# A decoder layer with sixteen experts: the expert stage reads its tiles' experts and names sixteen to a register load in place of four

## The chip, the cores and the metric

The kernel runs on one core of a Trainium2 chip. The metric is the device time of one execution in microseconds (us), the median of several runs, lower is better. Five engines work beside each other and meet at semaphores: TensorE (PE: matrix products; the profile lists its weight loads apart as PEld), VectorE (DVE), ScalarE (ACT), GpSimd (POOL) and SyncE (SP, which here only issues transfers). Each has a sequencer that takes its instructions in order. Instructions that work on registers are carried out by the sequencer itself and are not counted as busy time; the profile lists them for a line of the kernel under PEldq and SPq.

## The reference

One decoder layer over 2048 rows of width 256, in float32, with a layer norm after each of three parts:

```python
x = _layernorm(x + attention(x))                 # linear attention, 8 heads
x = _layernorm(x + cross_attention(x, ctx))      # 16 heads, 1601 keys
x = _layernorm(x + ffn(x))                       # mixture of experts
# ffn:
probs = softmax(xf @ gate_w.T)                   # 16 experts
top_w, top_idx = top_k(probs, 4);  top_w /= sum(top_w)
h1 = einsum('td,ehd->teh', xf, w1);  h3 = einsum('td,ehd->teh', xf, w3)
eout = einsum('teh,edh->ted', silu(h1) * h3, w2)
moe_out = einsum('ted,te->td', eout, combine)    # combine: the four weights of a row
shared = silu(xf @ sw1.T) * (xf @ sw3.T) @ sw2.T
out = moe_out + shared
```

## The kernel before

Attention and cross attention take the first 750 us of the trace. The change is in what comes after, the expert stage.

**Tiles.** The 2048 x 4 choices are sorted by expert into tiles of 128 rows, `SLOT_TILES` = 79 of them, which a row of DRAM (`sorted_d`) holds. Which expert a tile belongs to is known only on the chip. VectorE works out an order of the tiles and writes for each place in it two integers, the place of the expert's weights in `w_all` and the name (number) of the tile. They go through DRAM into `order_row`, on one partition of on-chip memory, in two versions: version 0 is complete for the first 48 places (`KNOWN_OWNERS`), version 1 for all.

**Work.** `WORK` is a fixed list of 95 items: 16 tiles of the shared expert ("s") and the 79 expert tiles ("e", place v): `"s"*4 + "e"*8 + "se"*6 + "e"*65 + "s"*6`. Every engine walks through it by the same index i, with a software pipeline. TensorE does at step i, in this order: a job of the last rows' attention and gate, if `LAST` has one for this i; `turn_rows(i+3)` (two transposes of the tile's rows, line 1601); `inner(i+1)` (products with w1 and w3, line 1639); `turn_act(i-1)` (one transpose, line 1647); `outer(i-3)` (product with w2, line 1657). For a place v that is a multiple of `EXPERT_LOAD`, `inner` first calls `load_owners(v)`, which reads `EXPERT_LOAD` integers of `order_row` into registers of TensorE with the instruction TENSOR_LOAD (line 1611). With four to a load that is at 20 places: v = 0, 4, ... 76, the last with three integers. The products then address the weights by register (`bass.ds(owners[v] + n, 1)`), for which the sequencer runs a FUSED_REGOPS for each. `inner(i)` waits for two things ahead of that: the tile's transposed rows (`xT_copied`, from ScalarE) and the activations of item i-2 (`act_ready`, from VectorE, line 2180).

**ScalarE, VectorE, GpSimd.** ScalarE copies the transposes out (1141, 1155), takes silu of the first product (1145) and scales the result (1163); VectorE multiplies (2180); GpSimd scatters a tile's 128 result rows to `given_d` in DRAM (874). Later VectorE adds four given rows for each row, normalises, and the result is stored.

**SyncE.** It issues the loads of the expert tiles' rows, `load_tile(i+8)` at step i (`X_AHEAD`), 14 of them ahead of the loop, each addressed by a register (line 695). At places that are a multiple of `EXPERT_LOAD` it first reads as many tile names (`name_tiles`, line 671). The very first read, for v = 0, is at the last step of cross attention, ahead of the wait for the sorted rows (line 679). Into its 18 buffers (`X_SLOTS`) a tile may go only when the tile 18 places before it has been given out. From step 63 on SyncE issues the loads of the given rows too, and the stores.

Places and steps: v = 0 is item 4, v = 16 item 26, v = 32 item 42, v = 48 item 58, v = 64 item 74.

Of the kernel before, what the change touches and what calls it, by code (L numbers as in the profile page):

```python
# [112 lines left out]
ACT_SLOTS = 3  # L113
WHOLE_SILU = 10
X_AHEAD = 8
EXPERT_LOAD = 4
IDLE_PRODUCTS = 3
EK_RING = 4
XQ_RING = 2
# [17 lines left out]
assert SLOT_TILES <= LISTED <= P and X_SLOTS % Y_SIGNALS == 0 and Y_SLOTS % Y_SIGNALS == 0  # L137
assert len(WORK) == TILES + SLOT_TILES and KNOWN_OWNERS % EXPERT_LOAD == 0
assert LASTK > 0 and REST * TPC <= CHUNK and UNITS == PER_STEP * KT


def decoder_layer(nc, a, out):
    with ExitStack() as ctx:
# [369 lines left out]
        def _(sp):  # L513
# [152 lines left out]
            def name_tiles(v):  # L666


                n = min(EXPERT_LOAD, SLOT_TILES - v)
                sp.wait_ge(order_in, 16)  # L670
                _, got = nc.values_load_multi_w_load_instructions(
                    order_row[0:1, 0, v:v + n, 1], engines=[mybir.EngineType.SP], min_val=0, max_val=SLOT_TILES - 1,
                    skip_runtime_bounds_check_because="the order is a permutation of the tiles")
                for k in range(n):
                    tile_at[v + k] = got[k]
# [5 lines left out]
            def load_tile(i):  # L681
                kind, v = WORK[i]
                if kind == "expert":
                    if v % EXPERT_LOAD == 0 and v:
                        name_tiles(v)
# [548 lines left out]
        def _(pe):  # L1234
# [371 lines left out]
            def load_owners(v):  # L1606


                n, known = min(EXPERT_LOAD, SLOT_TILES - v), int(v >= KNOWN_OWNERS)
                pe.wait_ge(order_in, 16 * (known + 1))  # L1610
                _, got = nc.values_load_multi_w_load_instructions(
                    order_row[0:1, known, v:v + n, 0], engines=[mybir.EngineType.PE], min_val=0,
                    max_val=W_PARTS * (EXPERTS + W_GAP - 1),
                    skip_runtime_bounds_check_because="a count of experts, cut off at the last one")
                for k in range(n):
                    owners[v + k] = got[k]
# [6 lines left out]
            def inner(i):  # L1623
# [5 lines left out]
                else:  # L1629
                    if v % EXPERT_LOAD == 0:  # L1630
                        load_owners(v)
# [750 lines left out]
```

## Time and profile before

| | |
|---|---|
| median of 3 runs | 959.58 us (958.43 to 962.15) |
| span of the profiled execution | 955.3 us |
| TensorE busy in it | 896.6 us (94%) |
| expert stage | about 750 to 955 us |
| register loads | 20 on TensorE, 20 on SyncE |

The span runs from the first to the last instruction of the profiled execution and is the only time of it that is listed; 4.3 us of the median of the runs lie outside it. Times within the trace count from the start of the span. In the table of waits and in the timeline "idle before <- releaser" is the time an engine stood still and the instruction of another engine whose end let it go on.

### The profile page before, as it was taken

How to read it: one execution, taken by the hardware profiler on the slowest of the kernel's cores; microseconds unless marked ns; L12 is line 12 of the kernel's file. 1: busy time of each engine (PE TensorE's matmuls, PEld its weight loads, DVE VectorE, ACT ScalarE, POOL GpSimd, SP SyncE). 2: the span in 40 equal slices, each digit the busy share in tenths (PEclk: the TensorE clock that was granted, in tenths of full speed). 3: DMA queues.
4: the chain of work that ended last, by engine and by line, in shares of the span. 5: the costliest groups of instructions: out<-in, count | busy, mean ns of one | idle time of the engine just before them, and what ended most of it. 6: DMA issues, size and time to landing. Idle time of an engine off the chain costs nothing.

```text
span 955.3 us, 18981 instructions
## 1 busy us (share of the span) xinstructions
PE 896.6 (94%) x6843; PEld 514.1 (54%) x6843; DVE 710.7 (74%) x1138; ACT 660.4 (69%) x1491; POOL 303.4 (32%) x355
## 2 busy tenths in 40 slices
PE   9998999799999999999999999999989997889995
PEld 5776876344444444444444444444433475677874
DVE  5324879899999998989998989988897271311477
ACT  4434574268888888878888878876779763556654
POOL 1608886600000000210000200023444446555574
PEclk9999999979999999999999999999999999999997
DMA  9207847502343400100100100102335433344795
GB/s 323 80 1 143 128 129 130 126 25 89 94 136 116 129 15 23 30 9 25 31 9 23 31 8 25 30 25 79 102 120 164 127 116 127 109 136 155 240 305 184
DMA packets 69839, 93.07 MB, mean 97 GB/s; under 512 B 15254, under 2 KB 52632, under 8 KB 69686
## 3 DMA queue, kind: packets, MB, share of 16 engines
q1 hardware_dynamic: 62068, 70.06, 26.7%
q0 software_dynamic: 6928, 18.82, 5.2%
q10 hardware_dynamic: 752, 2.98, 1.9%
q8 instruction: 56, 0.92, 0.4%
q14 instruction: 35, 0.29, 0.1%
HBM read 50.34 MB, written 39.40 MB: 94 GB/s over the span
## 4 chain that ended last, share of the span: by engine, by line
PE 75%; DVE 13%; ACT 4%; issue 3%; another core or an unknown queue 2%; POOL 2%; DMA 1%; POOLq 0%; DVEq 0%; SPq 0%; ACTq 0%
PE psum L1456 20%; PE psum L1364 16%; PE psum L1442 9%; PE psum L1639 8%; DVE mpart L1813 8%; PE psum L1657 3%; PE psum L1288 2%; PE psum L1383 2%; PE psum L1253 2%; ACT region L1191 2%; PE psum L1601 2%; PE psum L1314 2%; PE psum L1416 2%; PE psum L1478 1%
## 5 line engine op out<-in xcount | busy, mean ns | idle before, releaser
L1191 ACT ACTIVATE region<-psum 128x512 f32<-128x512 f32 (+1 forms) x832 | 448.4, 610 | 99.4 <-PE psum L1442 83.0
L1813 DVE TENSOR_REDUCE mpart<-psum 128x2 f32<-128x1024 f32 x384 | 461.8, 1222 | 33.5 <-PE psum L1364 25.8
L1456 PE MATMUL psum<-region 128*32 128x256 f32 (+1 forms) x3120 | 249.2, 391 | 2.3 <-ACT numT L1087 0.7
L1364 PE MATMUL psum<-kstack,qstack 63*128 63x512 f32 (+1 forms) x1024 | 213.9, 445 | 14.7 <-DVE mpart L1813 12.5
L1364 PEld LDWEIGHTS psum<-kstack,qstack 63*128 63x128 f32 x1024 | 88.9, 185 | 184.0 <-issue 130.8
L1442 PE MATMUL psum<-qstack,kstack 64*128 64x512 f32 (+1 forms) x832 | 176.0, 409 | 0.8 <-DMA qstack<-max_d 0.4
L1456 PEld LDWEIGHTS psum<-region 128*32 128x32 f32 (+1 forms) x3120 | 62.0, 108 | 110.8 <-issue 81.6
L1442 PEld LDWEIGHTS psum<-qstack,kstack 64*128 64x128 f32 (+1 forms) x832 | 111.8, 182 | 17.1 <-ACT region L1191 11.8
L939 POOL TENSOR_TENSOR attnT<-num_c,den_c 128x512 f32<-128x512 f32 x7 | 9.0, 1280 | 324.5 <-DMA den_c<-den_d 324.5
L1639 PE MATMUL psum<-w_all,xT_in 128*128 x316 | 84.5, 390 | 16.2 <-DVE act_h L2180 15.7
L874 POOL DMA_INDIRECT given_d<-y_out,x_in x79 | 78.3, 991 | 63.6 <-ACT y_out L1163 45.2
L2180 DVE SCALAR_TENSOR_TENSOR act_h<-silu_h,psum 128x128 f32<-128x128 f32 x95 | 27.1, 286 | 92.5 <-ACT silu_h L1145 50.9
L1639 PEld LDWEIGHTS psum<-w_all,xT_in 128*128 128x128 f32 x316 | 54.4, 192 | 24.9 <-issue 20.5
L837 POOL DMA_INDIRECT sorted_d<-x_rows,slots x48 | 47.5, 990 | 36.8 <-PE psum L1442 27.0
L1145 ACT ACTIVATE silu_h<-psum 128x128 f32<-128x128 f32 x85 | 24.6, 289 | 46.5 <-PE psum L1639 32.5
L1141 ACT ACTIVATE xT_in<-psum 128x256 f32<-128x256 f32 x95 | 37.2, 393 | 16.7 <-PE psum L1601 13.4
L1657 PE MATMUL psum<-w_all,actT 128*128 x158 | 47.7, 384 | 0.0
L1163 ACT ACTIVATE y_out<-psum,x_in 128x256 f32<-128x256 f32 x79 | 38.3, 484 | 6.9 <-PE psum L1657 3.6
L1060 ACT ACTIVATE region<-psum,small 128x64 f32<-128x64 f32 x128 | 27.9, 331 | 15.2 <-DVE small L1824 15.0
L1809 DVE TENSOR_REDUCE mpart<-psum 128x8 f32<-128x528 f32 x32 | 22.6, 708 | 12.0 <-PE psum L1364 10.6
L1155 ACT ACTIVATE actT<-psum 128x128 f32<-128x128 f32 x95 | 27.4, 288 | 5.0 <-remote 2.7
L1601 PE MATMUL psum<-ident,x_in 128*128 128x128 f32 x158 | 30.6, 275 | 0.3 <-ACT x2T L1126 0.3
(291 smaller groups left out, 1010.9 us busy)
## 6 DMA issues: line engine op xcount, KB each, us to landing
x_in<-sorted_d SPq DMA_DIRECT2D x79, 129.0 KB
sorted_d<-x_in SPq DMA_DIRECT2D x6, 1548.0 KB, 8.0
given<-given_d SPq DMA_DIRECT2D x16, 512.0 KB
qstack<-qparts_d SPq DMA_DIRECT2D x96, 64.0 KB, 2.3
qparts_d<-region SPq DMA_DIRECT2D x8, 512.0 KB, 3.3
kparts_d<-region SPq DMA_DIRECT2D x4, 800.5 KB, 12.1
kstack<-kparts_d SPq DMA_DIRECT2D x6, 400.2 KB, 10.1
kstack<-kparts_d ACTq DMA_DIRECT2D x6, 400.2 KB, 14.3
```

The lines of the kernel that those rows point to most:

```text
L837: pool.indirect_dma_start(out=sorted_d[:, :], out_offset=bass.IndirectOffsetOnAxis(ap=slots[:, t, j:j + 1], axis=0), in_=row, in_offset=No ...
L874: pool.indirect_dma_start(out=given_d[:, :], out_offset=bass.IndirectOffsetOnAxis(ap=x_in[:, v % X_SLOTS, DIM:DIM + 1].bitcast(I32), axis= ...
L1141: act.activation(xT_in[:, i % 3, :], turn_bank("tile", i)[:, 0:DIM], ACT.Copy).then_inc(xT_copied, 1)
L1163: act.activation(y_out[:, v % Y_SLOTS, :], bank(2 + i % 2)[:, 0:DIM], ACT.Copy, scale=x_in[:, v % X_SLOTS, DIM + 1:DIM + 2]).then_inc(y_co ...
L1191: act.activation(prob[0:rows_of, s % 3, j, :], ring(n)[0:rows_of], ACT.Exp).then_inc(ring_read, 1)
L1364: mm = pe.matmul(bank(unit_bank(u) + side)[:, at * w:(at + 1) * w], qstack[rows_of, buffer(G), p, t * P:(t + 1) * P], kstack[rows_of, g * ...
L1442: pe.matmul(ring(n)[0:r], kstack[rows, g * PAIRS + p, kt * P:kt * P + r], qstack[rows, buffer(G), p, :], start=True, stop=True).then_inc(r ...
L1456: mm = pe.matmul(bank(NUM_BANK)[VW * j:VW * (j + 1), q], vals[0:r, g, kt, j, :], prob[0:r, s % 3, j, q], start=(kt == 0 and half == 0), st ...
L1601: mm = pe.transpose(turn_bank("tile", i)[:, k * P:(k + 1) * P], rows[:, k * P:(k + 1) * P], ident[:, :])
L1639: mm = pe.matmul(bank(6 + i % 2)[:, 0:2 * HID], xT_in[:, i % 3, k * P:(k + 1) * P], part_of(kind, v, k), start=(k == 0), stop=(k == DK - 1))
L1657: pe.matmul(bank(2 + i % 2)[:, 0:DIM], actT[:, i % ACT_SLOTS, :], part_of(kind, v, DK), start=True, stop=True).then_inc(y_done, 1)
L1813: dve.tensor_reduce(mpart[:, G % 2, qt, :, p, n], both, X, ALU.max).then_inc(max_read, 1)
```

## The change

One constant. `load_owners` and `name_tiles` take `n = min(EXPERT_LOAD, SLOT_TILES - v)` integers wherever v is a multiple of it, so TensorE and SyncE read at v = 0, 16, 32, 48 and 64, with 16, 16, 16, 16 and 15 integers. 48 is a multiple of 16 as of 4, so version 1 of the order is used from the same place on. Nothing else is moved.

```diff
@@ -113,7 +113,7 @@
 ACT_SLOTS = 3
 WHOLE_SILU = 10
 X_AHEAD = 8
-EXPERT_LOAD = 4
+EXPERT_LOAD = 16
 IDLE_PRODUCTS = 3
 EK_RING = 4
 XQ_RING = 2
```

## Rows read from the trace of the kernel before

**Rows 1.** The page: busy time of the engines
```profile
PE 896.6 (94%) x6843; PEld 514.1 (54%) x6843; DVE 710.7 (74%) x1138; ACT 660.4 (69%) x1491; POOL 303.4 (32%) x355
```

**Rows 2.** The page: shares of the chain that ended last, by engine
```profile
PE 75%; DVE 13%; ACT 4%; issue 3%; another core or an unknown queue 2%; POOL 2%; DMA 1%; POOLq 0%; DVEq 0%; SPq 0%; ACTq 0%
```

**Rows 3.** Waits of TensorE, 755 to 940 us (total, times, longest)
```profile
PE psum L1639 <- DVE act_h L2180: 15.7, 14, 4.1
```

**Rows 4.** Lines 1611 and 671 over the whole span (min/median/max ns)
```profile
L1611 PEldq TENSOR_LOAD <-order_row x20: 757/1147/1345, 762.6 to 925.6; - x20
...
L671 SPq TENSOR_LOAD <-order_row x20: 861/868/1216, 750.3 to 913.7; - x20
```

**Rows 5.** Line 1611, single loads, each in a window around it
```profile
L1611 PEldq TENSOR_LOAD <-order_row x1: 1188/1188/1188, 762.6 to 762.6; - x1
...
L1611 PEldq TENSOR_LOAD <-order_row x1: 1227/1227/1227, 813.9 to 813.9; - x1
...
L1611 PEldq TENSOR_LOAD <-order_row x1: 1219/1219/1219, 846.6 to 846.6; - x1
...
L1611 PEldq TENSOR_LOAD <-order_row x1: 1160/1160/1160, 875.2 to 875.2; - x1
...
L1611 PEldq TENSOR_LOAD <-order_row x1: 1345/1345/1345, 903.6 to 903.6; - x1
...
L1611 PEldq TENSOR_LOAD <-order_row x1: 988/988/988, 918.4 to 918.4; - x1
...
L1611 PEldq TENSOR_LOAD <-order_row x1: 757/757/757, 925.6 to 925.6; - x1
```

**Rows 6.** Line 1639 on the sequencer of TensorE, either side of a load
```profile
L1639 PEldq FUSED_REGOPS  x2: 51/53/55, 874.5 to 874.6; - x2
...
L1639 PEldq FUSED_REGOPS  x2: 51/53/55, 876.6 to 876.8; - x2
```

**Rows 7.** Timeline of TensorE: first products of the tile after a load
```profile
764.54 1.13 PE L1639 MATMUL psum<-w_all,xT_in 128*128 x4 [0.35 <-DVE act_h L2180]
...
815.43 0.82 PE L1639 MATMUL psum<-w_all,xT_in 128*128 x2
...
848.45 1.13 PE L1639 MATMUL psum<-w_all,xT_in 128*128 x4 [0.36 <-DVE act_h L2180]
...
875.99 1.03 PE L1639 MATMUL psum<-w_all,xT_in 128*128 x4
...
877.61 1.03 PE L1639 MATMUL psum<-w_all,xT_in 128*128 x4
...
879.75 1.13 PE L1639 MATMUL psum<-w_all,xT_in 128*128 x4 [0.35 <-DVE act_h L2180]
...
905.45 1.03 PE L1639 MATMUL psum<-w_all,xT_in 128*128 x4
```

**Rows 8.** Timeline of TensorE: its four longest idle times here
```profile
798.03 1.33 PE L1639 MATMUL psum<-w_all,xT_in 128*128 x4 [2.51 <-DVE act_h L2180]
...
812.25 1.89 PE L1639 MATMUL psum<-w_all,xT_in 128*128 x4 [4.15 <-DVE act_h L2180]
...
825.78 1.12 PE L1639 MATMUL psum<-w_all,xT_in 128*128 x4 [1.82 <-DVE act_h L2180]
...
856.98 0.48 PE L1639 MATMUL psum<-w_all,xT_in 128*128 x1 [1.76 <-DVE act_h L2180]
```

**Rows 9.** Windows after two of these: busy times by engine, PEclk, DMA share
```profile
798.80:802.20 3.40, 3.40 (x11) 2.62 (x10) 0.72 (x3) 1.52 (x5) 2.72 (x3) 0.50 0.23 79
...
812.50:815.90 3.40, 3.40 (x11) 2.56 (x11) 0.94 (x3) 1.42 (x6) 2.08 (x3) 0.50 0.12 46
```

**Rows 10.** Line 671 on SyncE, its first and its seventeenth load
```profile
L671 SPq TENSOR_LOAD <-order_row x1: 1062/1062/1062, 750.3 to 750.3; - x1
...
L671 SPq TENSOR_LOAD <-order_row x1: 865/865/865, 893.8 to 893.8; - x1
```

**Rows 11.** Line 679 on SyncE, the wait for sorted rows
```profile
L679 SPq EVENT_SEMAPHORE  x2: 17/22/28, 755.5 to 758.5; - x2
```

## The prediction

> **What bounds the kernel now.** I read the page first. TensorE is busy 896.6 of 955.3 us [rows 1], and three quarters of the chain that ended last are its own [rows 2]. The expert stage is no exception: a tile there takes 1.62 us, from 875.99 to 877.61 [rows 7], and between 755 and 940 us TensorE waits 15.7 us in all, each time ahead of the first product of a tile and each time by the profile for VectorE's activation [rows 3]. So whatever holds TensorE up in this stage lengthens the kernel one for one, and nothing that only relieves another engine can shorten it by more than those 15.7 us.
>
> The register loads are not in this busy time. They are found by their lines: 20 on TensorE, 0.757 to 1.345 us each, median 1.147, and 20 on SyncE, median 0.868 [rows 4]. The question is what a load of sixteen integers takes, and how much of one is hidden.
>
> **The price of a load.** The trace before has one load that isn't of four integers, the last one on TensorE, of three. It took 0.757 us, the load of four before it 0.988, and no load of four in the trace was shorter than that [rows 4, 5]. The difference is 0.231 us for one integer, and 0.757 / 3 is 0.252: the time is nearly proportional to the integers, with next to nothing left for the instruction (0.757 - 3 x 0.231 = 0.064). SyncE's median of 0.868 is 0.217 for each. From this, sixteen integers cost on TensorE at least 0.064 + 16 x 0.231 = 3.8 us, and at most four times what the loads of four took at these places, 4.6 to 4.9 us (4 x 1.160 to 4 x 1.227) [rows 5]. I take 4.3, and 4.0 for the fifteen at v = 64; on SyncE 4 x 0.868 = 3.5. So the change takes away no load time worth the name: 79 integers are read either way. It gathers them in five blocks. The other end of what one short sample allows is a price for the instruction alone, 1.15 us whatever it reads; that is a rival below.
>
> The Trainium skill bears on this twice and says two things. "Runtime: NRT & Kernel Launch" (Instruction fetch mechanics) puts such a load at about 200 ns for each register, in bulk too; an estimate from it is 16 x 0.2 = 3.2 us a load, and the slope above and SyncE's 0.217 agree with it. "DMA: Bandwidth & Descriptors" (Latency and other measured facts) gives it a floor of about 600 ns and says that the compiler reads four at once to amortize that; by that rule sixteen at once would be better still, and the 0.064 us left over above speaks against it.
>
> **How much of a load is hidden.** TensorE's sequencer runs ahead of its array by the instructions that are queued. For v = 48: the load starts at 875.2 [rows 5], while the array is about to start the products of the tile before (875.99), and the next tile's products start at 877.61 without idle time [rows 7]. The sequencer's FUSED_REGOPS for those products come at 876.6 [rows 6], 0.26 us behind the load's end (875.23 + 1.16 = 876.39), and the one for the tile before came at 874.5, so the array could have waited until about 0.1 us before 877.61. The load could thus have lasted 2.0 us (877.61 - 875.23 - 0.26 - 0.1) before the array went idle: the 1.16 us are hidden, the 4.3 us are not. What hides a load is the sequencer's lead of about a tile and a half, and this can't grow, as the next tile but one has to wait for the activation of the one just computed.
>
> For each of the five loads, the start of the next products becomes load start + load time + 0.36, and the delay is what this lies behind its start now [rows 5, 7]:
> - v = 0: the four weight waits behind the load make it about 0.5 in place of 0.36: 762.6 + 4.3 + 0.5 = 767.4 against 764.54: 2.9
> - v = 16: 813.9 + 4.66 = 818.5 against 815.43: 3.1
> - v = 32: 846.6 + 4.66 = 851.3 against 848.45: 2.9 (0.36 of idle time stands there already)
> - v = 48: 875.23 + 4.66 = 879.9 against 877.61: 2.3, of which some 0.5 is taken back, since the next tile now waits at 879.75 [rows 7] and then no longer would: 1.8
> - v = 64: 903.6 + 4.0 + 0.36 = 908.0 against 905.45: 2.6
>
> The sum is 13.3 us. With 3.8 and 3.6 us a load it is 10.9, with 4.9 and 4.6 it is 16.3. Queued behind a load on TensorE is everything of the stage, from the last rows' attention on (the load at v = 0 comes ahead of their gate), and ScalarE, VectorE and GpSimd wait for it tile by tile; nothing catches up later, because the tiles that follow run at TensorE's own rate.
>
> **What the fifteen loads that go give back.** Hidden loads are worth nothing. Exposed, they can only be in the 15.7 us. Of these, 2.51 and 4.15 us end at 798.03 and 812.25 [rows 8], ahead of the loads at 799 and 813.9, and no load stands in them. The rest is 9.0 us, and that is the upper bound. 1.82 and 1.76 of it [rows 8] and ten waits that together make 5.5 us follow a load by some microseconds, with VectorE named as the releaser and not the sequencer. Whether the load has a part in them the trace doesn't settle. I take back half of the 5.5, 2.5 us (bounds 0 and 9.0).
>
> **The clock.** After the waits of 2.51 and 4.15 us the array ran at half its clock (granted 0.50, the 1.2 GHz level) for 3.4 us each time [rows 8, 9], which costs about 1.7 us; no fall follows the wait of 1.82 us. The new idle times, 2.3 to 3.3 us, lie just where it begins to happen. I put in one fall out of five, 1.7 us (bounds 0 and 5 x 1.7 = 8.5).
>
> **SyncE.** Its first load (v = 0) starts at 750.3 [rows 10] and the wait for the sorted rows ends at 758.5 [rows 11]: 3.5 us are hidden there. The three loads at v = 4, 8, 12 go from between the first tiles' transfers; TensorE doesn't stand still for a tile's rows there [rows 3], so that gains nothing. At v = 64 SyncE's load is at 893.8 [rows 10], TensorE's for the same place at 903.6 [rows 5]: 9.8 us ahead. It gets 2.6 us longer, and the transfers issued behind it, rows of tiles, given rows and stores, come 2.6 us later once. The lead hides it; if it were gone it would cost up to 2.6 us. No transfer is added or dropped, and fifteen short waits for the order go with the loads, all long satisfied.
>
> **Sum.** 13.3 - 2.5 + 1.7 = 12.5 us on a span of 955.3, so 967.8; with the 4.3 us that lie outside the span, 972 us against the median of 959.6 (+1.3%).
>
> **The rivals.**
> 1. *A load costs per instruction, not per integer.* Then five loads of 1.15 us stay hidden, fifteen go, and the kernel is faster by what they cost: 0 to 9 us, at best 950.6, likely 956 to 959. For it: loads of the same four integers vary from 0.988 to 1.345 us, so that one of 0.757 might be chance, and it is the only one. Against it: it lies outside this whole range on the side it should. It decides from where sixteen integers take less than about 2.0 us. Chance 0.13. The floor that the skill's page on DMA states is this rival's rule.
> 2. *Per integer, but mostly absorbed.* The waits for VectorE's activation come in bursts that don't depend on the loads, and a blocked sequencer lets ScalarE and VectorE catch up, so that a new idle time takes in old ones: of 13.3 us the 9.0 and no clock loss: +4, 964. For it: the wait at v = 48. Against it: ten of the waits are short, and only those beside one of five places can be taken in. Chance 0.15.
> 3. *The loads are split.* If the sixteen come out as four loads in a row, the profile has twenty again and the change doesn't do what it says. They stand in the same five places, though, so the time is that of the forecast; the chance (0.1) is inside the forecast's.
> 4. *Worse than the sum.* The clock falls each time, or SyncE's 3.5 us reach TensorE: 972 + 6.8 + 2.6, 981. Chance 0.07.
>
> **How the numbers follow.** Forecast 0.65, rivals 0.13, 0.15, 0.07. Forecast's own range: 10.9 - 5 to 16.3 + 3.4, so +6 to +20, 966 to 979. For 8 in 10 it reaches to rival 2 and into the gap below it, 960, and to rival 4, 980; left out are rival 1 and the worst of rival 4. About 0.5% (4.8 us) is what a measurement of this kernel can tell from no change. Slower by more than that: nearly all of the forecast and of rival 4 and some of rival 2, 0.76. Within it: most of rival 2, and rival 1 where the loads were hidden anyway, 0.17. Faster: 0.07.
>
> **What the profile after would show.** Line 1611 with five loads of 3.8 to 4.9 us (the last a sixteenth shorter) and line 671 with five of about 3.5: the price. In front of the first products of v = 0, 16, 32, 48 and 64 idle time of 2 to 3.3 us, with 1.62 us from tile to tile between: the exposure. Fewer short waits for the activation elsewhere would show that the loads had a part in them, the same number that they hadn't. Windows of half clock behind the five places: the clock. The prediction is wrong if the loads take under 2 us, or if the idle times are there and the stage still ends at 940.

## The result, and the profile after

The changed kernel takes 971.07 us (median of 4 runs, 963.36 to 974.43) against 960.3 us of the kernel before (4 runs, 958.43 to 962.15): ratio 1.0104, interval 1.0074 to 1.0134. The forecast was 972 against 959.6. Two more measurements of the same program, below, gave 1.0134 (1.0106 to 1.0163) and 1.0149 (1.0132 to 1.0166); by these ratios it is 10 to 14 us slower (by the medians 10.8, 12.5 and 15.2).

First the loads by their lines, which answer to [rows 4, 5] (min/median/max ns, first and last start in us), over the whole span and one by one:

```profile
L1611 PEldq TENSOR_LOAD <-order_row x5: 4014/4117/4661, 763.3 to 907.3; - x5
...
L671 SPq TENSOR_LOAD <-order_row x5: 3270/3622/3845, 751.4 to 897.0; - x5
...
L1611 PEldq TENSOR_LOAD <-order_row x1: 4014/4014/4014, 763.3 to 763.3; - x1
...
L1611 PEldq TENSOR_LOAD <-order_row x1: 4206/4206/4206, 817.9 to 817.9; - x1
...
L1611 PEldq TENSOR_LOAD <-order_row x1: 4117/4117/4117, 850.9 to 850.9; - x1
...
L1611 PEldq TENSOR_LOAD <-order_row x1: 4078/4078/4078, 879.0 to 879.0; - x1
...
L1611 PEldq TENSOR_LOAD <-order_row x1: 4661/4661/4661, 907.3 to 907.3; - x1
```

Five in place of twenty, each about four times as long. Then the timeline of TensorE, the first products behind each of them (start, duration, instruction, idle time ahead and what ended it), which answer to [rows 7], with the two tiles ahead of v = 48:

```profile
767.75 0.56 PE L1639 MATMUL psum<-w_all,xT_in 128*128 x1 [2.78 <-issue]
...
822.33 0.95 PE L1639 MATMUL psum<-w_all,xT_in 128*128 x2 [3.24 <-issue]
...
855.30 0.91 PE L1639 MATMUL psum<-w_all,xT_in 128*128 x3 [2.50 <-issue]
...
878.18 1.03 PE L1639 MATMUL psum<-w_all,xT_in 128*128 x4
879.81 1.03 PE L1639 MATMUL psum<-w_all,xT_in 128*128 x4
883.39 1.13 PE L1639 MATMUL psum<-w_all,xT_in 128*128 x4 [1.79 <-issue]
...
912.25 1.12 PE L1639 MATMUL psum<-w_all,xT_in 128*128 x4 [2.56 <-issue]
```

The releaser is "issue": the profile names no other engine, the array stood because its own sequencer gave it nothing. 2.78 + 3.24 + 2.50 + 1.79 + 2.56 is 12.9 us. The distance from tile to tile is still 1.63 us (878.18 to 879.81). The waits of TensorE, 755 to 950 us (total, times, longest; compare [rows 3]):

```profile
PE psum L1639 <- issue: 13.9, 7, 3.2
PE psum L1639 <- DVE act_h L2180: 5.6, 4, 3.2
PE psum L1657 <- ACT y_out L1163: 1.5, 2, 1.1
PE psum L1601 <- ACT xT_in L1141: 1.1, 1, 1.1
```

The waits for VectorE's activation are 5.6 us in place of 15.7. That looks as if having fewer loads had given 10 us back; the experiments show that this isn't the reason. The profiled execution is also the fastest of the four runs, with a span of 961.3 us. Its time is 963.36 us, so 2.1 us lie outside the span and not the 4.3 us that were taken above from a span and a median of other executions. The sum's 12.5 us is not touched by that. Between the two profiled executions the span rose by 6.0 us, half of the sum; between the medians the time rose by 10.8 us.

### The profile page after: what moved, and what is told of

Read it like the earlier page. It is cut to its first block, busy times and chain, and to the rows that moved or that the text cites. A ratio compares the mean times of both kernels' runs of the same rounds, so it can differ in the third digit from the quotient of the medians.

```text
span 961.3 us, 18951 instructions
## 1 busy us (share of the span) xinstructions
PE 896.1 (93%) x6843; PEld 513.9 (53%) x6843; DVE 710.8 (74%) x1138; ACT 663.6 (69%) x1491; POOL 303.5 (32%) x355
## 4 chain that ended last, share of the span: by engine, by line
PE 76%; DVE 12%; issue 4%; ACT 3%; POOL 2%; DMA 2%; another core or an unknown queue 1%; POOLq 0%; SPq 0%; DVEq 0%; ACTq 0%
PE psum L1456 20%; PE psum L1364 16%; PE psum L1442 9%; PE psum L1639 8%; DVE mpart L1813 7%; PE psum L1657 4%; PE psum L1288 2%; PE psum L1383 2%; PE psum L1253 2%; PE psum L1601 2%; PE psum L1314 2%; PE psum L1416 2%; PE psum L1478 1%; POOL x_rows L816 1%; PE psum L1647 1%
## 5 line engine op out<-in xcount | busy, mean ns | idle before, releaser
L1364 PE MATMUL psum<-kstack,qstack 63*128 63x512 f32 (+1 forms) x1024 | 213.8, 445 | 14.5 <-DVE mpart L1813 12.3
L1442 PEld LDWEIGHTS psum<-qstack,kstack 64*128 64x128 f32 (+1 forms) x832 | 111.9, 182 | 17.2 <-ACT region L1191 11.2
L1141 ACT ACTIVATE xT_in<-psum 128x256 f32<-128x256 f32 x95 | 36.5, 385 | 12.5 <-PE psum L1601 8.7
L1060 ACT ACTIVATE region<-psum,small 128x64 f32<-128x64 f32 x128 | 27.9, 331 | 15.2 <-DVE small L1824 15.1
L1383 PE MATMUL psum<-region 128*128 128x256 f32 x128 | 30.8, 384 | 0.0
## 6 DMA issues: line engine op xcount, KB each, us to landing
kparts_d<-region SPq DMA_DIRECT2D x4, 800.5 KB, 12.3
```

What stands on the lines that cost most here:

```text
L1364: mm = pe.matmul(bank(unit_bank(u) + side)[:, at * w:(at + 1) * w], qstack[rows_of, buffer(G), p, t * P:(t + 1) * P], kstack[rows_of, g * ...
L1383: mm = pe.matmul(bank(3)[:, 0:DIM], qsT[:, t % 2, f * P:(f + 1) * P], fold[:, f, :], start=(f == 0), stop=(f == SF - 1))
L1442: pe.matmul(ring(n)[0:r], kstack[rows, g * PAIRS + p, kt * P:kt * P + r], qstack[rows, buffer(G), p, :], start=True, stop=True).then_inc(r ...
```

## The experiments

All times are compared with the kernel before in runs on the same chip. Twelve runs follow, the first of them a repeat.

**The changed kernel again, and with its idle times filled.** The first is the yardstick. The second queues six products on TensorE ahead of the transposes that precede each of the five loads:

```diff
+FILL = 6
 ...
+                if i - 2 >= 0 and WORK[i - 2][0] == "expert" and WORK[i - 2][1] % EXPERT_LOAD == 0:
+                    for _ in range(FILL):
+                        pe.matmul(turn_bank("tile", i)[:, 0:DIM], ident[:, :], w_shared[:, 0, :], start=True, stop=True)
```

> The changed kernel again, beside the three runs of this call. Both theories: about +10 us on the kernel before (ratio 1.010), with five idle times of 1.8 to 3.2 us ahead of the products behind the loads. It is the yardstick for the version with filler products.

> The changed kernel with six products of 128x256 float32 that nobody reads queued on TensorE ahead of each of the five loads (2.6 us of array time each), so that the array works while its sequencer reads. They take the place of idle time and change no result. Theory A, the stalls cost their own idle time alone: the filler fills what was idle, the time is that of the changed kernel or up to 3 us more. Theory B, falls of the clock behind the idle times cost a large part (the timed runs have a mean clock of 0.968 to 0.973 where the profiled one has 0.985): the mean clock comes back to 0.984 and the time falls by 4 to 8 us below the changed kernel's.

The repeat took 970.08 us against 957.62, ratio 1.0134. The filled one took 967.13 us, ratio 1.010 (1.0073 to 1.0127), 3 us less than the repeat although its array does nearly 14 us more work (the products take 2.75 us ahead of a load). The granted clock differs between the two. Windows (length, busy times by engine, PEclk, DMA share, GB/s) behind the loads at v = 16, 32 and 64, first in the repeat, then in the filled kernel, at the same times:

```profile
819.80:826.60 6.80, 5.11 (x14) 3.89 (x15) 2.68 (x11) 2.23 (x8) 3.12 (x4) 0.50 0.24 80
857.40:860.80 3.40, 3.40 (x12) 2.65 (x11) 0.29 (x1) 1.45 (x5) 0.95 (x1) 0.50 0.54 41
915.40:918.80 3.40, 3.40 (x11) 2.61 (x10) 1.29 (x5) 1.30 (x4) 0.95 (x1) 0.50 0.76 267
```

```profile
819.80:826.60 6.80, 5.88 (x30) 4.86 (x29) 2.15 (x10) 1.82 (x6) 4.82 (x5) 1.00 0.40 129
857.40:860.80 3.40, 3.40 (x20) 2.87 (x19) 0.58 (x2) 2.10 (x8) 0.96 (x1) 1.00 0.51 38
915.40:918.80 3.40, 2.05 (x13) 1.56 (x12) 0.30 (x2) 0.90 (x4) 0.00 (x0) 1.00 0.75 251
```

Granted 0.50 is the 1.2 GHz level, 1.00 the 2.4 GHz level. Behind three of the five loads, after idle times of 4.07, 3.21 and 2.25 us, the repeat ran at half clock for 3.4 to 6.8 us, and behind v = 0 and v = 48, after 2.92 and 1.80 us, it did not; the filled kernel did behind none. Over all runs of this series the mean clock was 0.971 to 0.975 in those of the changed kernel (mean 0.973), 0.975 to 0.984 in those of the kernel before (0.979) and 0.978 to 0.984 in those of the filled kernel (0.982). From 0.979 to 0.973 over 965 us is 2 x 0.006 x 965 = 12 us more at half clock, worth up to 6 us where the array sets the pace. Not all of it need lie in the expert stage: the traces show 13.7 to 34.1 us of half clock ahead of the first load, whatever the kernel. Theory B's direction holds and its size (4 to 8 us) doesn't, as far as this test can say: the filler has a cost of its own. It delays the tile's transposes: the two waits below (the filled kernel, behind v = 48 and v = 64) are for ScalarE's copy of them:

```profile
886.78 1.13 PE L1643 MATMUL psum<-w_all,xT_in 128*128 x4 [0.88 <-ACT xT_in L1142]
...
917.03 1.12 PE L1643 MATMUL psum<-w_all,xT_in 128*128 x4 [1.35 <-ACT xT_in L1142]
```

So 3 us is what filling gave back net in this pair, and the two intervals still overlap a little.

**One engine at a time.** A second constant for SyncE's reads (`NAME_LOAD` in `name_tiles` and `load_tile`):

```diff
-EXPERT_LOAD = 4
+EXPERT_LOAD = 16        # the other kernel: 4
+NAME_LOAD = 4           # the other kernel: 16
```

> Sixteen at a time on TensorE alone, four on SyncE. Theory A (TensorE's blocked sequencer is the cause): the same time as the changed kernel, +9 to +11 us on the kernel before. Rival (SyncE's longer blocks delay the tiles' transfers): no more than a third of that.

> Sixteen at a time on SyncE alone, four on TensorE. Theory A: within 1 us of the kernel before, SyncE's loads of 3.3 to 3.8 us are hidden by its lead of some ten us. Rival: +5 us or more.

TensorE alone: 967.11 us, ratio 1.0097 (1.0064 to 1.013). SyncE alone: 957.44 us, ratio 1.0000 (0.9983 to 1.0017). The loss is TensorE's; SyncE's loads of 3.28 to 4.20 us are hidden. TensorE alone was 3 us below the changed kernel in this series, which might be a share of SyncE's when both are late, or the clock (0.976 against 0.973 on average). A later pair bears on it.

The second kernel also shows what the kernel before's waits are. It has the same twenty loads of four on TensorE, and here its waits from 755 to 950 us are:

```profile
PE psum L1640 <- DVE act_h L2181: 6.9, 6, 2.9
PE psum L1640 <- issue: 3.9, 1, 3.9
```

6.9 us for VectorE with unchanged loads, against 15.7 in the kernel before (755 to 940 us in [rows 3], and the same up to 950). How much stands under VectorE's name varies from trace to trace with the same loads on TensorE; the total idle time varies less, as the table at the end of this section shows.

**Fewer integers to a load.** The same two constants, at 8/8, 2/4, 1/4 and 1/1 (TensorE/SyncE):

```diff
-EXPERT_LOAD = 4
+EXPERT_LOAD = 8         # 2, 1, 1 in the others
+NAME_LOAD = 8           # 4, 4, 1
```

> Eight at a time on both. Price per integer: ten loads on TensorE of about 2.1 us (half of 4.1), each just at the 2.0 us that the sequencer's lead hides, so idle times of 0 to 0.5 us behind them and a time within 2 us of the kernel before. Price per instruction and something: loads well over 2.1 us.

> Two at a time on TensorE, four on SyncE. Price per integer: forty loads of about 0.5 us, all hidden. If the waits for VectorE's activation in the kernel before (15.7 us) have nothing to do with its loads, the time is that of the kernel before within 1 us; if the loads of four have a part in them, it is 2 to 6 us faster.

> One at a time on TensorE, four on SyncE. Price per integer: 79 loads of 0.25 to 0.3 us, one ahead of each tile, all hidden; the time is as with two at a time. If an instruction had a price of its own of 0.6 us or more, 79 loads of 0.6 us would still be inside the lead, but would show in the load's row.

> One at a time on TensorE and on SyncE. As one at a time on TensorE alone, within 1 us: SyncE's reads of 0.22 us lie in its lead.

Line 1612 is the load on TensorE in these kernels; the rows in the order 8, 2, 1:

```profile
L1612 PEldq TENSOR_LOAD <-order_row x10: 1855/2100/2408, 764.0 to 915.6; - x10
```

```profile
L1612 PEldq TENSOR_LOAD <-order_row x40: 375/526/1122, 765.9 to 931.6; - x40
```

```profile
L1612 PEldq TENSOR_LOAD <-order_row x79: 298/305/710, 765.5 to 928.1; - x79
```

The times:

| integers, TensorE / SyncE | loads on TensorE | median ns | us (before, same series) | ratio | interval |
|---|---|---|---|---|---|
| 1 / 1 | 79 | 306 | 958.82 (957.1) | 1.0021 | 1.0006 to 1.0035 |
| 1 / 4 | 79 | 305 | 957.58 (957.1) | 1.0009 | 0.9996 to 1.0023 |
| 2 / 4 | 40 | 526 | 956.54 (957.1) | 0.9993 | 0.998 to 1.0007 |
| 8 / 8 | 10 | 2100 | 955.55 (957.1) | 0.9981 | 0.9968 to 0.9993 |

Per-integer pricing holds in all of them. With two to a load (median 0.526 us) the kernel is as fast as with four: the loads of four had no measurable part in the 15.7 us. Eight to a load is level with or slightly better than four; 1 / 1 is slightly worse. Eight were not fully hidden, though: in the trace of 8 / 8 the array stands idle beside seven of the ten loads, 0.2 to 1.2 us each where at most 0.5 was expected, 5.5 us in all. The longest of these:

```profile
817.23 1.12 PE L1640 MATMUL psum<-w_all,xT_in 128*128 x4 [1.16 <-ACT xT_in L1142]
```

The kernel isn't slower for it.

**The blocked time doubled, twelve at a time, and two more pairs.**

```diff
 # doubled:
                     if v % EXPERT_LOAD == 0:
                         load_owners(v)
+                        load_owners(v)
 # twelve at a time:
-EXPERT_LOAD = 4
+EXPERT_LOAD = 12
```

> The changed kernel with each load on TensorE done twice, the second result used. The sequencer is blocked for 8.2 us at five places in place of 4.1. Theory A (a fixed lead of about 2.0 us hides the first part, everything behind it is idle time one for one): another 5 x 4.1 = 20.5 us, +31 to +36 us on the kernel before, and idle times of 6 to 7.3 us. If slack elsewhere absorbed part of the stalls, less than +25.

> Twelve at a time on both, seven loads. Price per integer, 0.05 + 12 x 0.253 = 3.1 us; less the lead of 2.0 us some 1.1 us of idle time at each of seven places (1.6 at the first), too short for the clock to fall. Theory A: +6 to +9 us. If the clock's falls were most of the changed kernel's loss: +4 us or less.

The doubling did not happen. The row of its profile says so, with five loads of the old length; that the first of two loads was dropped because nobody read its registers is my reading:

```profile
L1611 PEldq TENSOR_LOAD <-order_row x5: 3998/4263/4478, 766.5 to 915.2; - x5
```

So this is the changed kernel for a third time: 971.55 us against 956.35, 1.0149. It does not test what a longer block costs. But its trace shows that the lead is not fixed. The load at v = 16 started at 818.99, and the array went idle 0.3 us later (823.74 - 4.42 = 819.32):

```profile
823.74 0.79 PE L1640 MATMUL psum<-w_all,xT_in 128*128 x1 [4.42 <-issue]
```

Twelve at a time took 962.78 us, ratio 1.0069 (1.0054 to 1.0084), +6.6 us by the ratio, inside the +6 to +9 expected. The expectation that its idle times would be too short for the clock to fall was wrong: after 1.96 us (v = 0) and 2.19 us (v = 36) the array ran at half clock for 3.4 us, so this run doesn't separate idle time from the clock. Its loads:

```profile
L1611 PEldq TENSOR_LOAD <-order_row x7: 1814/3053/3070, 764.7 to 922.6; - x7
...
L1611 PEldq TENSOR_LOAD <-order_row x1: 1814/1814/1814, 922.6 to 922.6; - x1
```

The shortest is the last one, of seven integers (79 - 6 x 12). With the medians of the other kernels, 0.305 us for one, 0.526 for two, 2.100 for eight, 3.053 for twelve and 4.117 for sixteen, the line through one and sixteen is 0.051 + 0.254 for each integer; it gives 2.08 for eight, 3.10 for twelve and 1.83 for seven.

> Sixteen at a time on TensorE, four on SyncE, with the six filler products ahead of each of the five loads. Beside the version without filler (+9.3 us in its call): if the clock's falls cost what the other filler version suggested, +6 to +7 us and a mean clock of 0.983; if that gain of 3 us was chance, +9 us.

> Eight at a time on TensorE, four on SyncE. Loads of 2.1 us, just hidden: within 2 us of the kernel before, and like eight on both (-1.6 us) if it is TensorE's part that made that one faster.

The first is the filler and the two constants of above together (16 / 4): 966.45 us, ratio 1.0101 (1.0086 to 1.0116), mean clock of its runs 0.979 to 0.983. It does not confirm a gain of 3 us beside 16 / 4 without filler (1.0097): with SyncE's four the filler gained nothing, though it held the clock. What it adds is that with the filler SyncE's sixteen and four are equal (1.0100, 1.0101). The second (8 / 4): 956.74 us, ratio 1.0004 (0.9995 to 1.0014), within 2 us of the kernel before, but not below it. The 0.2% of eight on both is not shown to be TensorE's part.

**The stage in all the traces.** From the start of the first load on TensorE to the end of its last product with w1 and w3, one trace for each run: how long that is, for how much of it the array stood idle (idle times over 0.15 us), how much of this began beside a load (between its start and 0.6 us behind its end), and for how long it ran at half clock.

| integers to a load on TensorE | traces | us | idle | of it beside loads | half clock |
|---|---|---|---|---|---|
| 1 to 8 | 7 | 174.1 to 178.4, mean 175.7 | 12.3 to 16.9, mean 15.1 | 0.3 to 6.8 | 0 to 13.7, mean 4.9 |
| 12 | 1 | 180.4 | 17.5 | 7.2 | 13.7 |
| 16 | 4 | 183.6 to 189.6, mean 185.8 | 20.4 to 23.0, mean 21.7 | 11.8 to 17.2 | 6.8 to 20.5, mean 16.2 |
| 16, with filler | 2 | 184.4, 185.1 | 15.0, 13.3 | 4.9, 4.8 | 0, 6.8 |

The stage gets 10.1 us longer with sixteen. Its idle time grows by 6.6 us and not by the 11.8 to 17.2 us that stand beside the loads: what is idle elsewhere shrinks from 11.9 to 14.3 us (one to four integers to a load) to 5.8 to 9.8 us. The other 3.5 us go with 11.3 us more at half clock, which can cost up to half of that, 5.7 us. With filler the added idle time and most of the half clock are gone, and the nearly 14 us of filler stand in their place.

## Why the prediction was right

**The price of a load.** Right. Taken from one load of three beside one of four, 0.231 us an integer and 0.064 left over, it measured 0.254 and 0.051; I took 4.3 us for sixteen, it was 4.1. For the fifteen at v = 64 I had 4.0 and an upper bound of 4.6; it was 4.66. That bound was four times the other places' loads and left out that the load of four at this very place took 1.345 us [rows 5], which gives 5.0 (1.345 x 15 / 4). Rival 1, a price per instruction, is out: sixteen take 3.6 times as long as four in the trace before (4.117 / 1.147). Of the two rules weighed, the one on some 200 ns a register in "Runtime: NRT & Kernel Launch" (Instruction fetch mechanics) of the Trainium skill, stated there for loads from HBM, is near the measured 0.226 of SyncE (3.622 / 16) and 0.254 of TensorE. The other, a floor of about 600 ns in "DMA: Bandwidth & Descriptors" (Latency and other measured facts) of the Trainium skill, does not show here: loads of one took 0.305 us.

**What is hidden.** Right in the sum for one trace; the fixed lead is not. In the trace after, the idle time begins 1.7, 1.2, 1.9, 2.6 and 2.4 us behind the five loads' starts (for v = 48: 883.39 - 1.79 = 881.60, against 879.04), where I had 2.0. The rest of a load and 0.27 to 0.49 us behind its end are idle time: 12.9 us, where the sum had 13.3. In the three other traces with sixteen on TensorE and no filler it begins 0.3 to 2.6 us behind the load's start, and the sums are 11.8, 14.2 and 17.2 us.

**What comes back.** A size that was off, and for another reason than mine. I took 2.5 us for the fifteen loads that go, within bounds of 0 and 9.0 (the range then used 5 in place of 9.0, which no row gives). Two integers to a load, where every load has cover to spare, changed the time by 0.7 us (-1.9 to +0.7): what the loads of four cost was between nothing and 2 us. The 10 us that one pair of traces seems to show are mostly the scatter of those waits, as the kernel with unchanged loads on TensorE shows (6.9 us). What does come back is what rival 2 said: new idle times take in old ones, and "nothing catches up later" was wrong. Over the traces the idle time of the stage grows by 6.6 us (21.7 - 15.1), where the sum had 10.8 (13.3 - 2.5). Rival 2's time of 964 was that of the fastest, profiled execution; its "no clock loss" doesn't hold in the others.

**The clock.** Also a size. I put in one fall of five, 1.7 us. The profiled execution had two, behind v = 0 and v = 16 (0.50 in both windows), and as many as the kernel before had from its own waits [rows 9], so they don't show in the difference of the two pages:

```profile
768.00:771.40 3.40, 3.40 (x11) 2.56 (x11) 1.28 (x5) 0.77 (x3) 0.00 (x0) 0.50 0.45 131
822.60:826.00 3.40, 3.40 (x11) 2.62 (x11) 0.71 (x2) 0.82 (x3) 1.92 (x2) 0.50 0.47 155
855.40:858.80 3.40, 3.40 (x19) 2.89 (x20) 0.57 (x2) 1.80 (x7) 1.44 (x2) 1.00 0.67 105
```

The other three runs had 0.968 to 0.973, and that goes with their 971 to 974 us against 963. The traces of the changed kernel and of 16 / 4 put the clock at some 3.5 us of the stage's 10.1, twice my 1.7; this is what the idle time leaves over, not a test, and the filler, which isn't free, says 3 us net in one pair and nothing in the other. So the forecast came out in part by luck: the idle time was taken about 4 us too high and the clock about 2 us too low.

**SyncE.** Right, 1.0000 for its part alone. Whether its sixteen cost something when TensorE reads sixteen too is not settled: 3 us in one pair, none in the pair with filler.

## What to carry to other kernels

A register load costs by the integer here, and what decides is not how many loads there are but how long one blocks the sequencer: blocks of up to some 2 us cost nothing that the times show; beyond that the array stands idle until shortly after the load's end. What that costs is less than the new idle time where old idle time is taken in, and more where the clock falls. From one to eight integers nothing changes by more than 0.2%; twelve cost 0.7%, sixteen 1.0 to 1.5%. So cut such loads to the time that the array's queued work covers, and measure this cover from the load's start to where the array goes idle, in more than one execution: it was 0.3 to 2.6 us here. Waits under one engine's name that vary between traces from 7 to 16 us should be seen in a second execution before a change is credited with them, and total idle time is the better measure.

## What the runs showed of the hardware

TENSOR_LOAD on TensorE: 0.305, 0.526, 2.100, 3.053 and 4.117 us for 1, 2, 8, 12 and 16 integers, some 0.254 us each and almost nothing for the instruction. The length of an idle time alone doesn't tell whether the granted clock falls behind it. Beside the loads 2.50 us (the changed kernel, v = 32) and 2.92 us (its repeat, v = 0) had no fall behind them; 2.78 and 3.24 us (the changed kernel) and 2.25 us (its repeat, v = 64) had one of 3.4 us each. So had 1.94 us in the kernel with sixteen on TensorE and four on SyncE (v = 64, half clock from 915.7):

```profile
915.10 1.52 PE L1640 MATMUL psum<-w_all,xT_in 128*128 x4 [1.94 <-issue]
```

Runs of one program differed by 11 us (963 to 974), with mean clocks of 0.985 and 0.968. With products that nobody needs ahead of the loads the clock did not fall behind any of them, which was worth 3 us at best.
